# Layer 2's expert stage on routed blocks of rows, and where its weights and the pooled layer's weights are loaded

## The reference

```python
def _moe(tokens, router_w, w1, b1, w2, b2):          # layer 2: 625 rows, 8 experts, top 2
    logits = tokens @ router_w.T
    probs = softmax(logits)
    rw, re = top_k(probs, 2)
    rw = rw / maximum(rw.sum(-1, keepdims=True), 1e-12)
    combine = zeros((N, E)).at[arange(N)[:, None], re].set(rw)
    out = tokens
    for e in range(8):
        h = gelu(tokens @ w1[e] + b1[e])             # 256 -> 256
        y = h @ w2[e] + b2[e]                        # 256 -> 256
        out = out + combine[:, e:e + 1] * y
    return out

x = x + _L2_ffn_ref(_layernorm(x), ...)
x = x + _L3_gnn_ref(_layernorm(x), edge_index, ...)  # graph layers on 625, 313, 157 nodes, and back up
```

## Time and profile before

| | us |
|---|---|
| three runs | 968.25, 974.82, 975.25 |
| median | 974.82 |
| the profiled execution, whole | 974.79 |
| its span, first to last instruction | 972.7 |
| PE busy in the span | 897.7 |
| DVE, ACT, POOL busy | 441.9, 281.4, 181.6 |

### The profile page before, as it was taken

The page is one execution under the profiler, slowest core; times in us unless marked ns, Lnnn a source line. Parts: engine busy times, 40 slices in busy tenths (PEclk is TensorE's granted clock), DMA queues, the critical chain, the costliest instruction groups (busy, mean ns, idle before and its releaser), DMA issues.

```text
span 972.7 us, 15315 instructions
## 1 busy us (share of the span) xinstructions
PE 897.7 (92%) x5575; PEld 725.7 (75%) x5575; DVE 441.9 (45%) x1403; ACT 281.4 (29%) x625; POOL 181.6 (19%) x177
## 2 busy tenths in 40 slices
PE   7999998999999999898996778999999999899798
PEld 7998656889999777788875667777887654565665
DVE  6688665522222421632278976423435142340623
ACT  5110263122222114233337863333111111114300
POOL 2100000122221200045427751000101100000231
PEclk9999999999999999999988979999998899799899
DMA  8203001388885603159251000353100000321596
GB/s 313 123 1 91 1 0 26 109 295 316 313 317 214 238 0 130 53 192 323 91 162 71 1 1 1 130 179 119 59 1 7 26 1 1 130 77 53 193 348 240
DMA packets 28001, 120.34 MB, mean 124 GB/s; under 512 B 5401, under 2 KB 10032, under 8 KB 20132
## 3 DMA queue, kind: packets, MB, share of 16 engines
q1 hardware_dynamic: 22362, 104.39, 30.2%
q0 software_dynamic: 5280, 14.95, 4.6%
q10 hardware_dynamic: 295, 0.14, 0.1%
HBM read 106.11 MB, written 13.36 MB: 123 GB/s over the span
## 4 chain that ended last, share of the span: by engine, by line
PE 76%; DVE 13%; issue 4%; DMA 3%; ACT 2%; POOL 1%; SPq 0%; DVEq 0%; POOLq 0%; ACTq 0%
PE PS L800 8%; PE PS L464 6%; PE PS L618 5%; PE PS L815 5%; PE PS L432 5%; PE PS L867 4%; PE PS L851 4%; PE PS L476 4%; PE PS L543 4%; PE PS L1251 3%; PE PS L942 3%; PE PS L931 3%; PE PS L891 2%; DVE ring L1961 2%; PE PS L1032 2%
## 5 line engine op out<-in xcount | busy, mean ns | idle before, releaser
L432 PE MATMUL PS<-const 128*128 128x128 f32 x674 | 89.5, 292 | 5.8 <-DVE X L1341 2.1
L432 PEld LDWEIGHTS PS<-const 128*128 128x128 f32 x674 | 85.1, 206 | 10.1 <-DVE X L1341 2.9
L800 PE MATMUL PS<-HT,ring 128*128 128x128 f32 x680 | 79.1, 275 | 3.3 <-DVE HT L1495 1.7
L800 PEld LDWEIGHTS PS<-HT,ring 128*128 128x128 f32 x680 | 78.4, 192 | 4.6 <-issue 3.9
L2621 POOL TENSOR_TENSOR col<-col,power 125x4 f32<-125x4 f32 (+2 forms) x13 | 11.9, 918 | 311.1 <-DVE col L1334 225.5
L2681 POOL DMA_INDIRECT slot_rows<-ST,route x41 | 41.5, 1011 | 151.2 <-ACT ST L2395 95.9
L2719 POOL TENSOR_TENSOR arena<-arena,ring 125x625 f32<-125x625 f32 x40 | 55.7, 1416 | 34.2 <-ACT arena L2483 30.0
L1881 DVE TENSOR_TENSOR HT<-HT,PS 128x256 f32<-128x256 f32 (+1 forms) x51 | 19.1, 377 | 89.8 <-ACT HT L2384 71.6
L618 PE MATMUL PS<-HT 125*125 125x250 bf16 x470 | 51.5, 270 | 0.0
L618 PEld LDWEIGHTS PS<-HT 125*125 125x125 bf16 x470 | 50.3, 136 | 0.1
L1032 PE MATMUL PS<-w,HT 125*64 125x125 f32 x400 | 30.3, 305 | 18.0 <-DVE w L1980 18.0
(11 more groups left out here) (469 smaller groups left out, 1704.1 us busy)
## 6 DMA issues: line engine op xcount, KB each, us to landing
ring<-in_experts SPq DMA_DIRECT2D x17, 1386.0 KB
ring<-in_experts SPq DMA_DIRECT2D x17, 768.0 KB, 5.9
ring<-in_experts SPq DMA_DIRECT2D x11, 1026.0 KB
arena<-in_experts SPq DMA_DIRECT2D x10, 1024.0 KB
ring<-in_experts SPq DMA_DIRECT2D x7, 1024.0 KB, 8.9
arena<-in_experts SPq DMA_DIRECT2D x6, 1026.0 KB
arena<-in_gnn SPq DMA_DIRECT2D x5, 1024.0 KB, 5.8
ring<-in_experts SPq DMA_DIRECT2D x8, 513.0 KB, 3.7
```

The source lines that it names most:

```text
L432: pe.matmul(PS[:, bank, 0:128], ident, ident, start=True, stop=True)
L800: mm = pe.matmul(PS[:, bank, at:at + SLOTS], both[:, j, k, m * 128:(m + 1) * 128], xs[0][i % 2][:, k, :], start=(k == 0), stop=(k == KD - 1))
```

## The change

Layer 2's experts use the routed form of layer 1. The two layers share one `routed_blocks` on PE, DVE and ACT, with the hidden width (`WIDTH`, four blocks of 128 in layer 1, two in layer 2) and the number of weight buffers as parameters. Layer 2 has ten weight buffers: two at the start of the ring's halves, two in `w0`, and six more in the ring behind the first two, which are free when the attention's `raw` rows are done. Loads 0 to 3 are issued before layer 2's attention, 4 to 7 inside it, 8 and 9 when the extra experts are known, and each of the others when the block nine before it is finished.

Layer 3's graph weights come in two groups: three fifths and the bias rows behind loads 10 to 13, and the last two fifths (used on the way back up, `gnn3_late`) when layer 3's first normalised tile is ready, since `arena` holds the gathered and returned rows until then. `w1_3` is loaded behind them, because `w0` now holds expert weights. The norms of the pooling weights (`wn`) are computed in layer 1's graph network. There are 50 fillers in front of layer 3 in place of 14. Several semaphores per layer become one with a base per layer.

```diff
-PICKS = {0: 2, 1: 2, 3: 1}
-PER = {0: SLOTS, 1: SLOTS, 3: SLOTS // 2}
+PICKS = {0: 2, 1: 2, 2: 2, 3: 1}
+PER = {0: SLOTS, 1: SLOTS, 2: SLOTS, 3: SLOTS // 2}
...
+HIDDEN = {1: HID1, 2: D}
+WIDTH = {L: h // 128 for L, h in HIDDEN.items()}
+SIZE2 = KD * D + KD * D + KD
...
+AHEAD = {0: 4, 1: 4, 2: 4, 3: 4}
+PICKED = {0: 1, 1: 2, 2: 2, 3: 0}
+BUFFERS = {1: 7, 2: 10, 3: 9}
+BASE = {L: sum(BLOCKS[M] for M in PICKS if M < L) for L in PICKS}
...
+        expert2 = ([view(ring_flat[b], 0, 128, SIZE2) for b in range(2)]
+                   + [view(w0, b * SIZE2, 128, SIZE2) for b in range(2)]
+                   + [view(ring_flat[b // 3], (b % 3 + 1) * SIZE2, 128, SIZE2) for b in range(6)])
...
             def layer2_moe():
                 transposes(XN, busy=20)
                 logits(XT, wv(wr, WR, "l2", KD), KD)
-                moe(2, 2, KD * D)
-                bias2(2)
+                places(2)
+                routed_blocks(2)
...
             def layer3_gnn():
-                pe.wait_ge(gnn3_in, 96)
+                pe.wait_ge(gnn3_in, 64)
...
-                    transposes(xin, rows_, busy=(14, 0, 0)[i])
+                    transposes(xin, rows_, busy=(50, 0, 0)[i])
...
+                    if i == 0:
+                        pe.wait_ge(gnn3_late, 32)
...
             def take_rows(L, i):
...
+                if L == 2:
+                    ins = dve.tensor_copy(xs[2][i % 2], PS[:, 7, 0:KD * 128].rearrange("p (k n) -> p k n", k=KD))
+                ins.then_inc(xs_taken, 1)
...
+                    if L == 2:
+                        link(dve.tensor_scalar(share, share, 1e-12, None, ALU.max))
...
+            def routed_blocks(L):
+
+                for i in range(BLOCKS[L] + 1):
+                    if PICKED[L] <= i + 1 < BLOCKS[L]:
+                        dve.wait_ge(xs_full, BASE[L] + i + 2)
+                        if i >= 1:
+                            dve.wait_ge(act1_full, (acted_before(L) + WIDTH[L] * i) // 2)
+                        take_rows(L, i + 1)
+                    if i:
+                        b = (i - 1) % AHEAD[L]
+                        dve.wait_ge(ys_full, BASE[L] + i)
+                        if i > AHEAD[L]:
+                            dve.wait_ge(ys_out[b], rounds(L, i - 1 - AHEAD[L]))
+                        dve.tensor_copy(ys[L][:, b, :], PS[:, 5 + (i - 1) % 2, 0:D]).then_inc(ys_taken, 1)
...
             def layer2_moe():
                 layer_norm(X, XN, True)
                 take_transposes(XT)
-                gating(2)
+                dve.memset(chosen[:, NT, :], 0.0)
+                routing(2)
                 link(dve.tensor_tensor(X[:, :, :], X[:, :, :], XN[:, :, :], ALU.add))
...
-                experts(2)
-                take_bias2()
+                routed_blocks(2)
...
             rstd()
-            rstd()
+            exchange(2)
             rstd_parts()
...
+            for i in range(4):
+                load2(i, i)
+            spread_logits()
+            sp.wait_ge(bent_ready, 7 * NT)
+            for i in range(4, 7):
+                load2(i, i)
+            sp.wait_ge(bent_ready, NX * NT)
+            load2(7, 7)
+            sp.wait_ge(xn_ready, 7 * NT)
+            rows_out(2)
+            sp.wait_ge(spill_ready, NTH[2] + 1)
+            for i in range(NX, BLOCKS[2]):
+                e = sp.value_load(spill_i[0:1, i - NX:i - NX + 1], min_val=0, max_val=NX - 1)
+                if i >= BUFFERS[2]:
+                    sp.wait_ge(ys_full, BASE[2] + i - BUFFERS[2] + 1)
+                load2(e, i)
+                if 10 <= i < 13:
+                    gnn3_part(i - 10, gnn3_in)
+                if i == 13:
+                    sp.dma_start(rows3, io["rows3"].broadcast_to([128, ROWS3.size])).then_inc(gnn3_in, 16)
+            rows_back(2)
+            sp.wait_ge(xn_ready, 7 * NT + 1)
+            for j in (3, 4):
+                gnn3_part(j, gnn3_late)
             sp.dma_start(w0[:, 0:KD * 1024], io["w1_3"]).then_inc(w1_3_in, 16)
-            experts(2, KD * D + 2 * D + 2)
```

More of the change, by code:

```diff
@@ L69, in arrived, with acted_before @@
                     for M in PICKS if M <= L and b < AHEAD[M])
+def acted_before(L):
+    return sum(WIDTH[M] * BLOCKS[M] for M in WIDTH if M < L)
 def loads(L, i):
@@ L1897, in layer1_gnn @@
                 take_transposes(XT)
+                for i in range(3):
+                    pw = poolw[0:TP, i * D:(i + 1) * D]
+                    ins = dve.tensor_tensor_reduce(XWE[:, i, 0:D], pw, pw, 1.0, 0.0, ALU.mult, ALU.add, wn[:, i:i + 1])
+                link(ins)
+                dve.tensor_copy(col[:, 3:NT], wn[:, 0:1].broadcast_to([TP, NT - 3]))
+                rstd(dve.tensor_copy(col[:, 0:3], wn))
+                link(dve.tensor_copy(wn, col[:, 8:11]))
                 for r in range(2):
@@ L2416, in layer1_gnn @@
                 feature_major(1, ACT.Relu, lambda m: ST[:, 1, :], lambda m: COLS(cols, "g_b2"))
-            def hidden(L, blocks, at):
-                hid = HT[:, 0:blocks * N].rearrange("p (m n) -> p m n", m=blocks)
-                act.sem_inc(hid_free[L], 4)
-                with act.Fori(0, NX // 2) as i:
-                    for b in range(2):
-                        for half, (c0, c) in enumerate(HALVES):
-                            for m in range(blocks):
-                                ch = (b * 2 + half) * blocks + m
-                                act.wait_ge(hid_full[L], i * (4 * blocks) + (ch + 1))
-                                act.activation(hid[:, m, c0:c0 + c], PS[:, ch % 4, 0:c], ACT.Gelu,
-                                               bias=ring[:, b, at + m:at + m + 1]).then_inc(hid_free[L], 1)
             def turn_comb():
```

351 lines of the change are left out of this document (126 added, 225 removed).

## The result

The changed kernel takes 981.3 us (median of 9 runs, 978.47 to 986.28); beside it the kernel before took 975.25 (9 runs). The ratio is 1.0072, with a 95% interval of 1.0042 to 1.0103. So the change made the kernel about 6 to 7 us slower, where 1.4 us less was forecast. That is inside the range (966 to 985) and within the 1% that was called "no change", but on the other side.

What follows compares the result with a forecast made beforehand. The prediction took TensorE (PE), busy 92% of the span, as the bound. Its terms, -70.1 - 10.1 + 59.1 (experts) + 19.7 (tail) = -1.4 us, gave 973.4 us from 974.82, range 966 to 985.

Steps and rivals of the forecast that it cites:

- Routing exposed: Layer 2, before its experts: routing, formerly hidden behind expert 0, puts the first gather 13.6 us behind the probabilities' normalisation.
- First scatter: Layer 2's first blocks: gather 2 landed and turned after 3.5 us, scatter 0 at 627.1 after a first gather at 621.7.
- Steady state: Layer 2's blocks: POOL 2.64 us per block if landing time L is under 4.2, otherwise three blocks per L + 3.68.
- clearly faster: Rival for layer 2's blocks: POOL takes only its 1.02 us per DMA, giving 962 us; chance 0.12.
- PE's order: Layer 2's blocks: down(j) stands behind block j+2's turning, so waiting for gather j+2 also holds block j's result and scatter.
- The landing L: Time until a layer 2 gather has landed: taken as 5 us until 651 and 3 after it.
- The recurrence: Layer 2's gathers and scatters stepped through: gather 16 at 659.8, last down ending at 666.6 instead of 677.57.
- The tail: From layer 2's last down to layer 3's first matmul: 19.7 us, 18.2 by the data alone; before 10.1.
- the burst: SP's loads beside layer 2's gathers from 621 on: expert loads, pooled parts and rows, 9.2 MB, done near 651.
- the POOL floor: Rival for layer 2's blocks: gathers land under 4.2 us, POOL's 2.64 us per block decides, 969.0 us; chance 0.12.
- Slower: Rival: SP's burst holds every layer 2 gather up for 8.5 us, giving 992 us; chance 0.13.
- Slow clock: Rival: PE at 1.2 GHz throughout layer 2's blocks, 3.96 us each, giving about 1003 us; chance 0.03.

Runs made afterwards that it cites:

- loads_late: Changed kernel with the whole burst (expert loads 8 on, pooled parts, rows) held until gather 2 has landed and been turned; 980.18 us, ratio to before 1.0045.
- down_first: Changed kernel with layer 2's down(i-1) ahead of the turning of block i+1 on PE, and DVE's copies reordered alike; 983.83 us, ratio to before 1.0100.
- after_again: The changed kernel run again without any edit, for a second profile; 982.68 us, ratio to before 1.0072.
- thin_again: Repeat of the changed kernel with expert loads 8 to 16 reused or cut to 64 KB and pooled parts and rows near 605 (timing only); 973.71 us, ratio 1.0002.

## Why the prediction was wrong

1. *Routing exposed.* Right: first gather 13.7 us behind the normalisation (13.6).
2. *First scatter.* Too short by 2.6 to 3.1 us. The term "3.5 until they are landed and turned" was taken from layer 1, where the row of gather 2 was no slower than 5.0; here SP's loads go out in the same microsecond. loads_late shows that without them the scatter comes 5.1 us behind the gather, as the 5.4 had it.
3. *Steady state.* The form was right: POOL's 1.32 both ways, and three blocks per landing plus 3.9 to 4.3 (3.68 forecast). So "clearly faster" fell by its own test. What failed in it is "with L under 4.2 POOL bounds": see the floor below. The step's remark on PE's order was right about what waits, and down_first shows that it was no fault to mend.
4. *The landing L.* This is the step that failed. "L = 5 until 651 and 3 after it" came as a median of 6.2 us for the gathers issued up to 652 and 3.8 for those behind (after_again), and those that PE waited for took 7.7, 6.3 and 5.5. The row of 8.5 us in layer 1 said so; it was weighed as one bad case, and L was set between the two shorter readings. The Trainium skill (DMA: Bandwidth & Descriptors, Anatomy of one DMA) gives about 2 us fixed plus the bytes, an estimate of 2.3 for a gather; here it was 2.6 to 3.9 beside light loads (loads_late, thin_again) and up to 7.8 at 400 GB/s, so here the rule comes near only where the queues are quiet.
5. *The recurrence.* 44.9 us forecast; 52.9, 56.6 and 58.2 measured. In after_again the excess of 8.0 is 2.7 until the first scatter, 2.1 until gather 7, 2.0 until gather 16 and 1.3 behind it. Its form holds: with after_again's own landings and first scatter put in, the same steps give some 51 us of the 52.9, an estimate. One slip is in it: scatter 1 should wait for gather 3 by step 3's rule, which with L = 5 is 630.4 and not 629.8.
6. *The tail.* Right: 19.4 in all three profiles (19.7), 18.4 by the data alone (18.2). XN is done at 698.05, 1.0 us before the filler ends.

What the burst costs can be set against its forecast. The forecast's own step from short landings (the POOL floor, 42.0 us for the stretch) to L = 5 (44.9) is 2.9 us; the runs without the burst price it at 7.2 us in time and 6 in the stretch. That is 4 of the 8 us by which the forecast was off. The other 4 or so are left when the burst is gone, and no step had them: with landings under 4.2 us the POOL floor promised 42 us for the stretch and 969.0 us in all, and 48.6 to 50.7 came, at the time of the kernel before. That the time still fell inside its range is owed to the width of the range. The floor had the right rate and the wrong time; the waits that no record explains are part of the reason, and the cause stays open. "Slower" had the right cause and too high a price (992). "Slow clock" came true in part as a clock (0.72 granted in the first 29 us of the first profile), not throughout, and not as a time.

## What to carry to other kernels

A transfer priced alone is priced for an empty queue: when a change starts gathers and bulk loads at one point, take the landing seen under the same fill, also for the very first gather, whose wait nothing covers. Where work in small blocks goes through GpSimd-issued DMAs, count these first: here 32 of them at 1.32 us each are 42 us, more than the 36 us that the prediction's matmuls alone promised. A load put off to relieve a queue needs its first waiter found by name, not its first use.

## What was not expected of the hardware

- Landing of a 131 KB gather: 2.6 to 3.9 us with the DMA engines at about 110 GB/s (thin_again), a median of 6.2 and up to 7.7 us at 345 GB/s (after_again, 620 to 652).
- A matmul group of 8 that starts behind a short wait took 1.13 us, against 0.89 when it follows other matmuls at the same granted clock of 1.00.
- Completions of matmuls seen by DVE 2 to 4 us behind the end in PE's record (thin_again: 634.64 and 637.43), in some profiles and not in others; cause open.
- The time of one kernel goes with its mean granted clock from run to run: the kernel before took 967.79 us at 0.970 and 979.95 at 0.949. The changed kernel's median clock was 0.951, that of the kernel before 0.956.
